# Row maxima carried to Q by DMA, value biases folded into the output projection's bias, the up projection in three passes, four units of exponentials kept

## The reference

```python
x = x + xattn(_layernorm(x), ctx, L0 weights)      # q, k, v, softmax over 256 keys, out @ Wo.T + bo
x = x + ffn0(_layernorm(x), ...)                   # W_exp, butterfly, gelu, butterfly, W_con
x = x + xattn(_layernorm(x), ctx, L1 weights)
x = x + moe(_layernorm(x), ...)                    # top 4 of 16 experts, silu(gate) * up, plus a shared one

# in xattn
attn = softmax(einsum('bhqd,bhkd->bhqk', q, k) / sqrt(8))
out  = einsum('bhqk,bhkd->bhqd', attn, v)
```

## Time and profile before

| what | us |
|---|---|
| median of 3 runs | 208.7 (208.29 to 209.09) |
| the profiled execution | 208.64 |
| its span in the trace | 206.8 |
| PE busy | 197.8 (96%) |
| DVE busy | 151.3 (73%) |
| ACT busy | 146.4 (71%) |
| POOL busy | 57.7 (28%) |

### The profile page before, as it was taken

How to read it: one execution, slowest core, us unless ns; L and a number is a source line. 1 busy time by engine, 2 the same in 40 slices (tenths; PEclk the granted TensorE clock), 3 DMA queues, 4 the chain that set the end, 5 groups by cost and what they waited for, 6 DMA issues and landing times.

```text
span 206.8 us, 4279 instructions
## 1 busy us (share of the span) xinstructions
PE 197.8 (96%) x1721; PEld 110.1 (53%) x1728; DVE 151.3 (73%) x240; ACT 146.4 (71%) x264; POOL 57.7 (28%) x74
## 2 busy tenths in 40 slices
...
GB/s 165 356 206 0 3 0 5 2 3 3 0 0 3 0 3 0 0 3 0 0 0 3 2 3 0 3 150 181 0 5 6 138 179 92 0 6 165 189 80 78
DMA packets 6084, 10.51 MB, mean 51 GB/s; under 512 B 1152, under 2 KB 3120, under 8 KB 5936
## 3 DMA queue, kind: packets, MB, share of 16 engines
...
...
## 4 chain that ended last, share of the span: by engine, by line
PE 84%; ACT 7%; DVE 5%; issue 2%; DVEq 0%; ACTq 0%
PE PS L362 63%; PE OB L362 21%; ACT P L866 3%; DVE T L1009 2%; DVE xn L997 1%; DVE Q L1018 1%; ACT sums L882 1%; ACT Q L837 1%; ACT o_raw L876 1%; ACT sums L885 0%; DVE x L1046 0%; DVE x L1053 0%; DVE sums L1033 0%; DVE attn L1039 0%; ACT K L832 0%
## 5 line engine op out<-in xcount | busy, mean ns | idle before, releaser
L1009 DVE TENSOR_REDUCE T<-PS 128x4 f32<-128x1024 f32 x64 | 76.6, 1220 | 7.7 <-PE PS L362 6.8
L866 ACT ACTIVATE P<-PS 128x512 f32<-128x512 f32 x128 | 68.2, 600 | 15.4 <-PE PS L362 15.3
L362 PE MATMUL OB<-P,V 128*32 128x256 f32 x512 | 33.8, 384 | 0.3
L766 POOL TENSOR_TENSOR attn<-o_raw,sums 128x512 f32<-128x512 f32 x5 | 6.4, 1284 | 91.4 <-ACT sums L885 91.4
L362 PE MATMUL PS<-K,Q 32*128 32x256 f32 x256 | 29.3, 323 | 0.8 <-DVE T L1009 0.3
L362 PEld LDWEIGHTS PS<-K,Q 32*128 32x128 f32 x256 | 18.1, 183 | 19.7 <-DVE T L1009 6.0
L362 PE MATMUL PS<-Q,K 32*128 32x256 f32 x256 | 27.1, 322 | 0.9 <-ACT P L866 0.7
L362 PEld LDWEIGHTS PS<-Q,K 32*128 32x128 f32 x256 | 17.1, 183 | 14.0 <-ACT P L866 7.3
L919 ACT ACTIVATE gate_t<-PS 128x512 f32<-128x512 f32 (+1 forms) x18 | 10.4, 596 | 18.2 <-DVE prod_t L1118 12.1
L362 PEld LDWEIGHTS OB<-P,V 128*32 128x32 f32 x512 | 14.3, 109 | 11.1 <-ACT P L866 1.1
L1118 DVE TENSOR_TENSOR prod_t<-PS,gate_t 128x512 f32<-128x512 f32 x16 | 10.9, 687 | 9.2 <-POOL hid_t L778 7.2
...
## 6 DMA issues: line engine op xcount, KB each, us to landing
spread<-comb_out SPq DMA_DIRECT2D x32, 128.0 KB, 3.0
...
x<-xT SPq DMA_DIRECT2D x2, 128.0 KB, 3.3
cx<-ctxT SPq DMA_DIRECT2D x2, 128.0 KB, 3.5
```

Of the source, the lines that this page charges most:

```text
L362: return nc.tensor.matmul(out, lhsT, rhs, start=start, stop=stop)
L766: finish(nc.gpsimd.tensor_tensor(attn[:, :, queries(b)], o_raw[:, k % 2, :].rearrange("p (a q) -> p a q", a=2), sums[:, k % 2, :].rearrang ...
L866: finish(nc.scalar.activation(P[:, (JOINT * U + j) % (JOINT * PUNITS), :, :].rearrange("p k q -> p (k q)"), PS[:, FILLED["sc", U, j // 2][ ...
L1009: finish(nc.vector.tensor_reduce(dst, two("max", U, i).rearrange("p j (t s) -> p j t s", t=2), AX.X, ALU.max, negate=True), "red", U, i)
```

## The change

- **Maxima.** `turn` and `shift` are gone from PE and DVE. `red.U.i` writes its four columns side by side into `T[:, U, 2i:2i+2, :]`, a tile with room for all units, and a new table `SP_ORDER` has a step `ld.U.i` for each of the 64: two DMAs, each of which takes 128 partitions x 2 elements of `T` into 256 elements of one row of `Q`. So that the order of elements fits, `max` now takes every second query as weights. `sc.U.i` waits for the two DMAs of its own half.
- **Value biases.** `vev` is a plain copy, split by layer into two steps of four instructions, one on DVE and one on ACT for each chunk. A new PE step `fb` (eight f32 instructions of one column) multiplies the biases with Wo, and `fbr` on DVE adds `BO`; `resid` uses the sum.
- **Up in three passes.** `w_up` is kept as f32r halves `w_up_hi` and `w_up_lo`; `uhi.c` (ACT) and `ulo.c` (POOL for c = 0, DVE for c = 1) split the normed x into `n_hi`, `n_lo`, and each `up.c.k` is three f32r matmuls.
- **P** holds four units.
- **The tables** are written anew. Beside the steps above: fills 16 with 43 matmuls (12 with 32 before); DVE has one K eviction, three Q evictions, three `xcopy`, three `hid` and one `nmul` more, two `fwr` and one `ocopy` fewer; ACT is the mirror of that for the evictions, copies and `fwr`, POOL for `hid` and `nmul`.

```diff
-TURNS = 2
-PUNITS = 3
+PUNITS = 4
+RING = 8
-max.3.1:12 turn.1:6 sc.0.0:03 fill.2:4 max.4.0:45 sc.0.1:12 fill.3:0 max.4.1:01 qsel.0.1.1:6 qsel.0.1.2:3
-qsel.1.0.3:0 max.17.1:45 centre.4:1 ksel.1.1.0:6 ksel.1.1.3:0 avg.4:2 turn.9:3 fill.3:4 sc.16.0:45 max.18.0:01
+out.0.1:5 max.16.0:01 fill.2:6 centre.4:6 max.16.1:45 max.17.0:01 avg.4:2 qsel.1.0.3:3 max.17.1:45 fill.2:6
+sc.16.0:06 max.18.0:12 fill.6:3 max.18.1:34 max.19.0:56 up.1.0:0 up.1.2:1 up.1.3:2 max.19.1:34 up.1.1:0
+SP_ORDER = """
+ld.0.1 ld.0.0 ld.1.1 ld.4.0 ld.2.0 ld.1.0 ld.2.1 ld.3.1 ld.5.0 ld.3.0 ld.4.1 ld.6.0 ld.6.1 ld.5.1 ld.7.0 ld.8.0
...
-        V = sb("V", [D, LAYERS, 2 * BATCH, 2, 8, 32])
+        with ExitStack() as first_values:
+            V0 = sb("V0", [D, 2 * BATCH, 2, 8, 32], stack=first_values)
...
-        T = sb("T", [D, TURNS, 2, D])
+        T = sb("T", [D, UNITS, JOINT, 2], f32r)
-        w_up = sb("w_up", [D, BLK, D])
+        w_up_hi, w_up_lo = (sb(n, [D, BLK, D], f32r) for n in ("w_up_hi", "w_up_lo"))
...
+        def turned_waited(eng, U, i):
+
+            if fresh(eng, turned_in[i][U % RING], 32 * (U // RING + 1)):
+                eng.wait_ge(turned_in[i][U % RING], 32 * (U // RING + 1))
...
                 for qt in range(2):
-                    q0 = b * SEQ + qt * D
+                    half = slice(b * SEQ + qt, (b + 1) * SEQ, 2)
                     for jj in range(2):
                         rows = slice(32 * (2 * i + jj), 32 * (2 * i + jj) + 32)
-                        last = mm(two("max", U, i)[:, jj, qt * SEQ:(qt + 1) * SEQ], Q[rows, g, q0:q0 + D],
+                        last = mm(two("max", U, i)[:, jj, qt * SEQ:(qt + 1) * SEQ], Q[rows, g, half],
...
-                after(pe, "shift", turned_with(U))
+                turned_waited(pe, U, i)
...
+            def three(to, w_high, w_low, high, low, start=True, stop=True):
+
+                mm(to, w_high, high, start=start, stop=False)
+                mm(to, w_high, low, start=False, stop=False)
+                return mm(to, w_low, high, start=False, stop=stop)
+
+            def fold(*at):
+
+                take()
...
+                for l in range(LAYERS):
+                    for a in range(2):
+                        last = mm(bank("fb")[:, l:l + 1], w_o[:, l, a, :], bvc[:, l, a:a + 1], start=a == 0, stop=a == 1)
+                give(last, "fb")
...
-                after(pe, "normed", norm(1, c))
+                after(pe, "ulo", c)
                 after(pe, "fwr", 3)
-                give(mm(bank("up", c, k), w_up[:, k, :], xn[:, chunk(c)]), "up", c, k)
+                give(three(bank("up", c, k), w_up_hi[:, k, :], w_up_lo[:, k, :], n_hi[:, :], n_lo[:, :]), "up", c, k)
...
+            def turn(U, i):
+
+                l, b, g = unit(U)
+                after(sp, "red", U, i)
+                if U >= RING:
+                    turned_waited(sp, U - RING, i)
+                for j in (2 * i, 2 * i + 1):
+                    sp.dma_start(Q[32 * j + g:32 * j + g + 1, g, queries(b)].bitcast(f32), T[:, U, j, :].bitcast(f32))\
+                        .then_inc(turned_in[i][U % RING], 16)
...
+            def high_rows(c):
+
+                after(act, "normed", norm(1, c))
...
+                finish(nc.scalar.activation(n_hi[:, :], xn[:, chunk(c)], ACT.Copy), "uhi", c)
...
-                dst = T[:, t % TURNS, :, :].rearrange("p t (j r) -> p j t r", r=32)[:, 2 * i:2 * i + 2, :, g]
-                finish(nc.vector.tensor_reduce(dst, two("max", U, i).rearrange("p j (t s) -> p j t s", t=2), AX.X,
+                finish(nc.vector.tensor_reduce(T[:, U, 2 * i:2 * i + 2, :], two("max", U, i).rearrange("p j (t s) -> p j t s", t=2), AX.X,
...
+                    link(nc.vector.tensor_copy(dst, src))
+                    finish(nc.vector.tensor_tensor(w_up_lo[:, :, :], src, dst.bitcast(f32), ALU.subtract), "fwr", step)
...
+            def low_rows(c):
+                after(dve, "uhi", c)
+                finish(nc.vector.tensor_tensor(n_lo[:, :], xn[:, chunk(c)], n_hi[:, :].bitcast(f32), ALU.subtract),
+                       "ulo", c)
```

More of the change, by code:

```diff
@@ L30 @@
 BANKS = 7
-TURNS = 2
-PUNITS = 3
+PUNITS = 4
+RING = 8
 SPREADS = 4
 BQ, BK, BO, BCON, BDOWN, BUP, ONES = 0, 2, 4, 6, 7, 8, 12
-TURNED = ((1, 1, 2),) + ((2, 2),) * 7
-TURN_UNITS = []
-for sizes in TURNED:
-    for size in sizes:
-        TURN_UNITS.append(tuple(sum(map(len, TURN_UNITS)) + i for i in range(size)))
-PE_ORDER = """
-fill.7:0 centre.0:0 kproj.0.0:1 avg.0:2 kproj.0.1:3 centre.1:4 fill.1:5 qproj.0.0:5 avg.1:6 ksel.0.1.3:0
-ksel.0.1.2:2 ksel.0.1.1:1 qsel.0.0.0:3 ksel.0.0.0:4 ksel.0.0.3:5 fill.3:0 max.0.0:34 qsel.0.0.1:0 ksel.0.0.1:6
@@ L59 @@
-avg.3:6 max.13.1:12 max.14.0:45 pv.9 sc.11.0:36 sc.11.1:12 turn.7:0 pv.10 sc.12.0:34 max.14.1:01 max.15.0:56
-up.0.1:2 up.0.3:4 max.15.1:01 up.0.2:5 up.0.0:6 sc.12.1:02 sc.13.0:14 pv.11 turn.8:5 down.0:6 sc.13.1:25
-sc.14.0:34 sc.14.1:01 centre.5:6 pv.12 avg.5:3 sc.15.0:05 sc.15.1:46 pv.13 pv.14 qproj.1.0:1 pv.15 ksel.1.1.1:2
-qsel.1.0.2:3 qsel.1.0.1:4 qsel.1.0.0:6 fill.6:0 max.16.0:01 max.16.1:45 fill.1:6 out.0.1:6 max.17.0:23
-qsel.1.0.3:0 max.17.1:45 centre.4:1 ksel.1.1.0:6 ksel.1.1.3:0 avg.4:2 turn.9:3 fill.3:4 sc.16.0:45 max.18.0:01
```

350 lines of the change are left out of this document (184 added, 166 removed).

## The result

The changed kernel takes 212.07 us (median of 4 runs, 211.5 to 212.5), the kernel before beside it 208.78 us (208.29 to 209.09): ratio 1.0162, 95% interval 1.0145 to 1.0179. It is slower, where 199.8 us was forecast. The profiled execution (212.5 us) has a span of 210.5 us.

A forecast was written before the change was run, and what follows sets the result against it. PE was taken to set the end, with 84% of the chain; -9.9 - 2.4 + 0.9 + 2.3 = -9.1, with 0.3 for the late `sc.16` -8.8, took 208.64 to 199.8 us; range 197.0 to 205.5.

The forecast's parts named there:

- The sum's items on PE: PE: `turn` gone -9.9 us, up -2.4, `fb` +0.9, fills +2.3, in all -9.1.
- The DMAs: 0 us on PE, if they are in time.: Maxima's 128 small transfers in the attention: issue no bound, landing 2.1 to 2.5 us, only `sc.16.0` up to 0.6 late.
- Rival 2: DMAs pace the attention, slower than before: some 220 us, or 212 if only landing is slow; chance 0.07.
- They lie on the chain, since PE is full, and count in whole.: 17 `turn` steps on PE at 0.58 us each: removing them shortens the kernel by the full 9.9 us.
- up to 1.5 us: First layer: DVE loses as much as PE, so PE's gain stands; this much against it in the range.
- near zero, at 71% busy: ACT: added value evictions, `fwr`, `uhi` and `ocopy` against some seven evictions and copies given up, net change near zero.
- Rival 1: Part of the gain given back in waits, DVE in the first layer being full: 203 to 205 us; chance 0.24.
- Up in three passes: -2.4 forecast: PE's `up` steps: 0.68 us each in three passes instead of 0.96 (chunk 0) and 1.03 (chunk 1), -2.4 us.
- Fills: +2.3 in the sum: PE: 43 fill matmuls instead of 32, 11 x 0.21 = 2.3 us, costing themselves or the wait they stand in.
- The tail behind the last `dn` and the start are as before: Kernel's start and its end behind the last `dn`: no change in time.

The follow-up runs named there:

- f1: Kernel of e4 with `w_up` as one f32 copy and each `up` one f32 matmul again, `uhi` and `ulo` gone: 205.66 us, ratio 0.9863.
- g1: Kernel of e4 with ACT's half of the value evictions issued twice, the first time into a spare tile: 205.8 us (2 runs).
- g2: Kernel of e4 with DVE's half of the value evictions issued twice: 206.25 us (2 runs).
- g3: Kernel of e4 with ACT's half of the second layer's value evictions (`vev.1.1`) moved to DVE: 206.6 us.
- e1: Changed kernel with the experts' weights loaded earlier, in the gap between the layers: 207.5 us, ratio to the kernel before 0.9958.
- e4: Changed kernel with the experts' weights loaded between the layers and the experts' steps in the order of before: 206.01 us, ratio 0.9887.
- e3: Changed kernel with the order of before from `sc.29.1` on, all engines, the weights' load left late: 210.5 us, ratio 1.0073.
- e7: e5 with three units in `P` instead of four: 214.9 us (1 of 4 runs), not settled.
- e5: All four edits of the change put by hand on the tables of before, experts' weights loaded between the layers: 214.8 us, ratio 1.0294.
- e6: e5 with the experts' weights loaded behind `nmul.1.0`, as in the kernel before: 213.75 us (2 of 4 runs), ratio 1.0234.

## Why the prediction was wrong

**The sum's items on PE stood nearly as forecast.** `turn` is gone from PE, `fb` takes 0.9 us (53.94 to 54.85), `max` and `sc` interleaved still 0.45 us, the reductions 1.22. DVE fell to 145.5, ACT stayed at 146.2. One term on PE was mis-sized: an `up` step in three passes takes 0.75 us (3.00 for four), not the 0.68 of the earlier trace rows, and one in f32 0.91 in f1, not 0.96, so chunk 0 gives 0.6 us instead of 1.1.

**The step that failed first: "The DMAs: 0 us on PE, if they are in time."** Landing was 2.0 us for one DMA, and the second of a pair is issued 0.64 us behind the first, so 2.6 us for a pair (I took 2.1 to 2.5, in a span of 2.1 to 3.5). Rival 2's fear of 8-byte pieces was not borne out; the issue is 0.60 us and not the 0.48 of the earlier trace rows, which had no effect that a run shows. What failed is the "if". I read from the earlier trace rows that the DMA engines are idle in the whole attention; those rows are the stretches from 20 and from 160 us. The weights of the experts are loaded at 135.86 in the kernel before, in the middle of the second layer's attention, and no line of the prediction has them. The new transfers share its engines, and it now comes 10 us earlier: `nmul.1.0`, which it stands behind on POOL, begins at 124.24, where that step began at 134.63 before. Of 128 transfers nine took 4.1 to 8.6 us, and one `sc` waited for them, 2.31 us. Rival 2 had the number (212) by slow landings, but in most units of the second layer; in the trace it was one `sc`, once, and 3.4 of the 5.7 us are the clock's. The number agreed by chance.

The Trainium skill (DMA: Bandwidth & Descriptors, Queues, rings and completion order) says that a DMA engine takes turns between its queues by packets. With up to 8.6 us from issue to landing for 1 KB during the load, the trace shows that taking turns did not keep the small transfer short. The read-modify-write below 512 B that the same page of the Trainium skill states (Specifications) did not bring the landing to the long end that I feared: 128 pieces of 8 bytes took 2.0 us when nothing large was under way. No run has the same transfer in larger pieces, so its own price is not shown.

**The second: "They lie on the chain, since PE is full, and count in whole."** PE was full and so were its neighbours. The share of 84% in the chain is a statement on the kernel as it ran, not on the next one. Up to pv.23 the steps at their distances give 8.7 us less, and 4.9 arrived; the missing 3.8 us lie in many small waits for exponentials and evictions, most at pv.0 to pv.4 (1.7 us; pv.4 comes no earlier than before), pv.8 to pv.12 (1.1) and at the change of layers (1.0). I had "up to 1.5 us" against DVE and "near zero, at 71% busy" for ACT. The average hid that ACT, the fourth of the engines listed, is at 7.91 and 9.09 from 60 to 80 us in the kernel before:

```profile
60.00:70.00 10.00, 9.87 (x116) 4.83 (x116) 7.20 (x11) 7.91 (x15) 0.00 (x0) 1.00 0.01 2
70.00:80.00 10.00, 10.00 (x71) 4.47 (x64) 5.62 (x8) 9.09 (x14) 0.49 (x1) 1.00 0.01 2
```

With `uhi`, an `ocopy` and its half of the value evictions it stands at 9.69 and 9.87. Rival 1 named this mechanism and its size, 3 to 5 us, for DVE; the traces of f1, g1, g2 and g3 show both engines.

**Up in three passes: -2.4 forecast, none measured at the end** (f1). The gain is on PE where ACT sets the pace.

**Fills: +2.3 in the sum.** Wrong in kind: I had said that they cost either themselves or the wait, and added them in whole. They stand in real waits: with 5.0 us of them taken away the kernel was not faster (206.5 and 208.9 us against 206.0). Had I priced them at nothing the sum would have been lower still, and further off, since the waits that they cover were not in it.

**The part I did not price at all: the experts' order.** "The tail behind the last `dn` and the start are as before" says nothing of the experts in between, whose steps the tables also move. From pv.31 on they take 5.0 us longer, of which the steps that moved behind pv.31 are a part; in whole the new order of the experts costs 1.5 us (e1 less e4; 2.0 in the traces), or 1.6 beside the late load (the changed kernel less e3; 2.5 in the traces).

The account: 212.07 less 4.5 for the collision (e1), less 1.5 for the experts (e4), is 206.0; of the 6.2 us from there to 199.8, 3.8 are the small waits of the attention up to pv.23, and they hold what the three passes were to bring; 1.8 lie between pv.28 and pv.31 (8.5 us against 6.7 before, for the same steps), where PE in e4 waits twice for 0.8 us. About 0.6 us is not accounted for. This last split is worked out from traces and not shown by a run each.

**What stays open.** Whether the fourth unit in `P` is worth anything (e7 and e5 overlap, and the new order does not run without it). What `turn` and `shift` are worth by themselves: no kernel had that edit alone. And when an idle PE loses its clock: 2.0 us did it in e5 and not in e6.
